# Sixteen transposes of a four-layer graph kernel: from TensorE to DMAs on ScalarE's queue

## What is computed

```
x = layernorm(x + L0(x, adj))   # adj @ (x @ W) + b, 8 heads of 32
x = layernorm(x + L1(x, adj))   # attention, 4 heads of 256
x = layernorm(x + L2(x, adj))   # two graph convolutions with relu
x = layernorm(x + L3(x, adj))   # relu(normalised adj @ x @ W)
# L1: ht = h @ W, src = ht . a_src, dst = ht . a_dst (per head)
#     e = leaky_relu(src[:, None] + dst[None, :]) + adj ; softmax(e) @ ht, mean of heads
```

## Time and profile before

| | us |
|---|---|
| median of 3 runs (lowest to highest) | 707.61 (707.03 to 707.86) |
| the profiled execution, its own time | 708.24 |
| its span on the core | 706.3 |
| PE busy in the span | 686.9 (97%) |
| DVE busy | 529.2 (75%) |
| ACT busy | 393.7 (56%) |
| POOL busy | 147.0 (21%) |
| mean granted clock of TensorE over the span | 0.995 |

### The profile page before, as it was taken

The page is one execution under the profiler, slowest core; times in us unless marked ns, Lnnn a source line. Parts: engine busy times, 40 slices in busy tenths (PEclk is TensorE's granted clock), DMA queues, the critical chain, the costliest instruction groups (busy, mean ns, idle before and its releaser), DMA issues.

```text
span 706.3 us, 16657 instructions
## 1 busy us (share of the span) xinstructions
PE 686.9 (97%) x5962; PEld 567.2 (80%) x5962; DVE 529.2 (75%) x988; ACT 393.7 (56%) x525; POOL 147.0 (21%) x236
## 2 busy tenths in 40 slices
PE   5989999999999999999999999999999999999996
PEld 4878854588888888888888888875677778888885
DVE  5788646999898979989899898998432325874564
ACT  6545146887989889798898989642100020123000
POOL 4965422000100000000000000653021102442222
PEclk9999999999999999999999999999999999999999
DMA  9986001001303012030300303013121000310011
GB/s 329 411 316 251 0 3 59 1 1 31 62 31 60 0 45 45 30 59 3 86 0 30 59 0 60 1 23 75 25 46 27 11 1 16 39 30 1 32 48 43
DMA packets 33147, 42.17 MB, mean 60 GB/s; under 512 B 21776, under 2 KB 27856, under 8 KB 30928
## 3 DMA queue, kind: packets, MB, share of 16 engines
q1 hardware_dynamic: 30528, 33.73, 14.8%
q0 software_dynamic: 2016, 7.34, 5.5%
q10 hardware_dynamic: 560, 0.52, 0.2%
HBM read 27.13 MB, written 2.13 MB: 41 GB/s over the span
## 4 chain that ended last, share of the span: by engine, by line
PE 84%; DVE 8%; POOL 4%; issue 1%; DMA 1%; ACT 1%; SPq 0%; POOLq 0%; DVEq 0%; ACTq 0%
PE ps L543 14%; PE ps L544 14%; PE ps L685 14%; PE ps L687 14%; PE ps L686 14%; PE ps L534 7%; PE ps L635 5%; DVE ring_hl L980 2%; DVE ring_a L975 2%; POOL x L1090 2%; POOL ring_a L1099 1%; DMA x<-in_x 1%; PE ps L499 1%; DVE x L753 1%; POOL ring_a L1111 0%
## 5 line engine op out<-in xcount | busy, mean ns | idle before, releaser
L687 PE MATMUL ps<-arena,ring_hl 128*128 (+1 forms) x1024 | 279.6, 273 | 0.0
L685 PE MATMUL ps<-arena,ring_hl 128*128 (+1 forms) x1024 | 278.8, 272 | 0.4 <-DVE ring_hl L980 0.4
L686 PE MATMUL ps<-arena,ring_hl 128*128 (+1 forms) x1024 | 278.6, 272 | 0.0
L543 PE MATMUL ps<-arena,adj 128*128 128x256 f16 (+1 forms) x1024 | 231.9, 273 | 0.6 <-issue 0.5
L544 PE MATMUL ps<-arena,adj 128*128 128x256 f16 x1024 | 232.1, 274 | 0.0
L975 DVE SCALAR_TENSOR_TENSOR ring_a<-rho,gam,ring_a 128x1024 f32<-128x1024 f32 x128 | 163.9, 1281 | 18.0 <-ACT ring_a L430 18.0
L980 DVE TENSOR_TENSOR ring_hl<-ring_a,ring_hl 128x1024 f16<-128x1024 f32 x128 | 156.7, 1224 | 6.0 <-ACT ring_hl L444 5.9
L444 ACT ACTIVATE ring_hl<-ring_a 128x1024 f16<-128x1024 f32 x128 | 135.3, 1057 | 44.2 <-PE ps L687 30.9
L430 ACT ACTIVATE ring_a<-adj,shift 128x1024 f32<-128x1024 bf16 x128 | 145.7, 1139 | 0.0
L543 PEld LDWEIGHTS ps<-arena,adj 128*128 (+1 forms) x1024 | 100.2, 98 | 18.5 <-issue 0.7
L544 PEld LDWEIGHTS ps<-arena,adj 128*128 (+1 forms) x1024 | 99.8, 97 | 16.4
(11 more groups left out here) (91 smaller groups left out, 566.8 us busy)
## 6 DMA issues: line engine op xcount, KB each, us to landing
arena<-in_adj SPq DMA_DIRECT2D x16, 1024.0 KB, 8.5
x<-y POOLq DMA_DIRECT2D x14, 512.0 KB, 5.2
rho<-s_scratch SPq DMA_DIRECT2D x8, 512.0 KB, 3.7
out_x<-x SPq DMA_DIRECT2D x16, 128.0 KB, 1.7
x<-in_x SPq DMA_DIRECT2D x3, 512.0 KB, 7.0
arena<-in_L_gnn_W SPq DMA_DIRECT2D x1, 1024.0 KB, 16.8
arena<-in_L_gnn_a SPq DMA_DIRECT2D x1, 1024.0 KB, 19.0
rho<-in_L_gnn_W SPq DMA_DIRECT2D x2, 512.0 KB, 10.2
```

The costliest lines, as they stand in the source:

```text
L543: nc.tensor.matmul(ps[:, bank, 0:width], lhs, pp[:, j, 0, 0:width], start=(j == 0), stop=False)
L685: nc.tensor.matmul(acc, hi, v_hi, start=(jt == 0), stop=False)
L686: nc.tensor.matmul(ps[:, b, 0:D], hi, v_lo, start=False, stop=False)
L687: ins = nc.tensor.matmul(acc, lo, v_hi, start=False, stop=(jt == T - 1))
```

## The change

The sixteen tiles of the second layer are no longer transposed on TensorE. ScalarE issues one DMA transpose for each tile, in order, each behind the low half of that tile's split, with one semaphore for each slot of `xs`; ScalarE's copies of the transposes are gone, and its casts stand between the issues (cast 7 ahead of the first one). TensorE's projections move from tile t - 5 to tile t - 7 in the steps of tile t (TURN_LAG = R + 3 = 7), so the aggregates of tiles 7 to 15 carry the projections of tiles 0 to 8, and seven are left, which go among the first six halves of the values as 1, 2, 1, 1, and one after each of the last two. VectorE's takes move from round t + 4 to round t + 7; those of tiles 9 to 15 stand after tile 15's split. VectorE's split of a tile waits for the DMA of four tiles before it in place of TensorE's transpose.

```diff
--- before.py
+++ after.py
@@ -154,6 +154,7 @@
         s_t, s_xt = sem("s_t"), sem("s_xt")
         s_td = sem("s_td")
         s_tc = [sem(f"s_tc{i}") for i in range(2)]
+        s_tg = [sem(f"s_tg{i}") for i in range(R)]
         s_w, s_ph, s_c = sem("s_w"), sem("s_ph"), sem("s_c")
         s_acc, s_sum = sem("s_acc"), sem("s_sum")
         s_deg, s_degp, s_dis, s_disw = sem("s_deg"), sem("s_degp"), sem("s_dis"), sem("s_disw")
@@ -211,10 +212,15 @@
             return adj[:, (n % 2) * JH:(n % 2 + 1) * JH, (n // 2) * LW:(n // 2 + 1) * LW], src
 
         EARLY = T - R - 1
+        TURN_LAG = R + 3
 
         def by_pe(k, t):
 
-            return k * T + t if k < 2 else 2 * T + (k - 3) * (T - EARLY) + t - EARLY
+            return t if k == 0 else T + (k - 3) * (T - EARLY) + t - EARLY
+
+        def gat_turned(t, u):
+
+            return s_tg[u], (t - u) * 4 + 16
 
         def conv_turned(t):
 
@@ -356,13 +362,12 @@
                     if t - AHEAD in between:
                         between[t - AHEAD]()
 
-            def lagged(k, first=0):
+            def lagged(k):
 
                 def one(t, u):
                     take_t(k, t, u)
-                    if k != 1:
-                        take_p(k, t, u)
-                tiles(act, first, T, one)
+                    take_p(k, t, u)
+                tiles(act, EARLY, T, one)
 
 
             def w1_hi(kk):
@@ -390,12 +395,14 @@
             nc.scalar.activation(w3[:, 0, :, :], w3f, ACT.Copy, scale=WS).then_inc(s_wh, 1)
             act.wait_ge(s_wa, 4 * K2)
             nc.scalar.activation(was[:, 0], wa[:, :, :, :], ACT.Copy, scale=WS).then_inc(s_wah, 1)
-            casts_after = {0: 7, 1: 9, 2: 11, 4: 13, 5: 15}
-            for t in range(R + 2):
-                take_t(1, t, t % R)
+            cast_n(7)
+            casts_after = {0: 9, 2: 11, 4: 13, 5: 15}
+            for t in range(T):
+                act.wait_ge(s_lo, T + t + 1)
+                act.dma_start_transpose(xt[:, t, :].rearrange("p (c i) -> p c i", c=2 * K2),
+                                        xs[:, t % R, :, :].rearrange("p q f -> p (q f)")).then_inc(s_tg[t % R], 16)
                 if t in casts_after:
                     cast_n(casts_after[t])
-            lagged(1, R + 2)
             act.wait_ge(s_turn, 1)
             act.wait_ge(s_wl, 3)
             nc.scalar.activation(srow, ps[0:SROWS, 7, 0:P], ACT.Copy).then_inc(s_sr, 1)
@@ -486,7 +493,7 @@
                 tiles(act, 0, EARLY - EARLY % R, lambda t, u: take_p(k, t, u))
                 for t in range(EARLY - EARLY % R, EARLY):
                     take_p(k, t, t % R)
-                lagged(k, EARLY)
+                lagged(k)
 
 
         @block.tensor
@@ -505,7 +512,9 @@
             def project(k, t, u):
                 if k == 0 and isinstance(t, int) and t == 0:
                     pe.wait_ge(s_wl, 1)
-                if k == 2:
+                if k == 1:
+                    pe.wait_ge(*gat_turned(t, u))
+                elif k == 2:
                     pe.wait_ge(*conv_turned(t))
                 elif k > 2 and not (isinstance(t, int) and t >= EARLY):
                     pe.wait_ge(s_td, by_dma(k, t))
@@ -579,17 +588,16 @@
             def rest(a, knext, ready):
 
                 k = (0, 2, 3, 4)[a]
+                back = TURN_LAG if knext == 1 else R + 1
 
                 def one(t, u):
                     pe.wait_ge(s_sum, t + (a * T - R + 1))
-                    prep = knext is not None and not (isinstance(t, int) and t == R)
+                    prep = knext is not None and not (isinstance(t, int) and t < back)
                     for j in range(T):
                         if j % JH == 0:
                             ready(t, u, j // JH)
-                        if j == T // 4 and prep and knext < 3:
-                            transpose(knext, t - R - 1, (u - 1) % R)
                         if j == (T - 2 if knext in (3, 4) else T // 2 + 2) and prep:
-                            project(knext, t - R - 1, (u - 1) % R)
+                            project(knext, t - back, (u - back) % R)
                         agg_step(a, k, t, u, j, j == T - 1)
                 one(R, 0)
                 tiles(pe, R + 1, T, one)
@@ -642,18 +650,16 @@
                     values_half(t, u, half)
 
             pe.wait_ge(s_wl, 5)
-            transpose(1, T - R - 1, R - 1)
-            transpose(1, T - R, 0)
-            for n in range(R):
+            left = list(range(T - TURN_LAG, T))
+            for n, count in enumerate((1, 2, 1, 1)):
                 pe.wait_ge(s_sum, T - R + n + 1)
                 values_half(n // 2, n // 2, n % 2)
-                project(1, T - R - 1 + n, (n - 1) % R)
-                if n < R - 1:
-                    transpose(1, T - R + n + 1, n + 1)
-            pe.wait_ge(s_xt, 2 * T - 1)
-            values_half(2, 2, 0)
-            project(1, T - 1, R - 1)
-            values_half(2, 2, 1)
+                for _ in range(count):
+                    tt = left.pop(0)
+                    project(1, tt, tt % R)
+            for n in range(2):
+                values_half(2, 2, n)
+                project(1, left[n], left[n] % R)
             pe.wait_ge(s_c, 2 * T)
             pe.wait_ge(s_idf, 1)
             nc.tensor.matmul(ps[0:SROWS, 7, 0:P], sd[:, 0, :, :].rearrange("p h t -> p (h t)"), ident_f[:, :],
@@ -808,8 +814,10 @@
 
                 def split():
 
-                    if k < 3:
-                        dve.wait_ge(s_t, t + (k * T - R + 1))
+                    if k == 1 and isinstance(t, int) and t < R:
+                        dve.wait_ge(s_t, T - R + t + 1)
+                    elif k == 1:
+                        dve.wait_ge(*gat_turned(t - R, u))
                     elif k == 3 and isinstance(t, int) and t < R:
                         dve.wait_ge(*conv_turned(t + T - R))
                     elif isinstance(t, int) and (t < R or t >= EARLY + R):
@@ -853,13 +861,14 @@
                     early, late_ = stages(a, k, t, u)[0], stages(a, k, t - 1, (u - 1) % R)[1]
                     if isinstance(t, int) and t == R:
                         late_ = []
-                    if k is not None and not (isinstance(t, int) and t == R and a > 0):
-                        late_.append(lambda: take(k, t - R, u))
+                    if k is not None and not (isinstance(t, int) and (t < behind or t == R)):
+                        late_.append(lambda: take(k, t - behind, (u - behind) % R))
                     if isinstance(t, int) and t in fill:
                         late_.append(fill[t])
                     for n in range(max(len(early), len(late_))):
                         for st in early[n:n + 1] + late_[n:n + 1]:
                             st()
+                behind = TURN_LAG if k == 1 else R
                 peeled = max(len(fill), 1)
                 for t in range(R, R + peeled):
                     one(t, t % R)
@@ -867,7 +876,7 @@
                 for st in stages(a, k, T - 1, R - 1)[1]:
                     st()
                 if k is not None:
-                    for t in range(T - R, T):
+                    for t in range(T - behind, T):
                         take(k, t, t % R)
 
             def sum_products(n):
```

## The result

| | before | after |
|---|---|---|
| median of 4 (lowest to highest), us | 707.74 (707.03 to 712.05) | 715.24 (712.08 to 717.31) |
| ratio to before, 95% interval | | 1.0094 [1.0075, 1.0113] |
| the profiled execution, its span | 708.24, 706.3 | 712.08, 710.1 |
| PE busy | 686.9 | 684.3 |
| mean granted clock | 0.995 | 0.992 |

Slower, as forecast, by more than forecast: the forecast was 712.0 in 709.3 to 714.2. The profiled execution is the fastest of the four. Thirteen executions of the changed kernel over several comparisons lie between 711.2 and 718.1, median 713.8; 69 of the kernel before lie between 706.9 and 712.1, median 708.4 (707.7 to 708.6 in the single comparisons). So two things ask for a reason: the step of 5.4 us between the medians, and a spread of 7 us.

A forecast was written before the change was run, and what follows sets the result against it. TensorE was taken to bound the kernel (84% of the chain), with VectorE's takes holding it after the change. Aggregates +0.7, tail +2.0 and clock +1.7 made 4.4 us: 712.6 profiled, 712.0 against the median, range 709.3 to 714.2.

The forecast's parts named there:

- The aggregates: Second layer's aggregates: projection 2 in tile 9 waits 6.2 us for VectorE's take 0; they end at 91.5, +0.7 us.
- No wait at 44: Sign in TensorE's timeline: the hole from about 44.2 to 46.5 us, before tile 0's transpose, goes, worth 2.3 us.
- The takes' order in the tail: Tail: projection 11 waits 1.5 us for take 9 behind tile 15's split; projection 15 starts 10.2 after the aggregates, +2.0 us.
- a fixed chain over VectorE, GpSimd and again VectorE: Tail, from projection 15 on: this chain frees the banks, and the values go on 5.2 us later.
- The clock: Behind the 6.2 us stand in tile 9 the clock falls: +1.7 us, bounds 0 and 2.6.
- the 475 to 480 row: Profile row of a stand of about 2.3 us that left the clock at 1.00, cited against a loss of clock.
- the clock falls twice: Rival: a second clock fall in the tail, behind stands of 1.5 and about 1.6 us; 1.7 more, 713.7; chance 0.13.
- The DMA lands late: Rival: tile 15's landing in the tail takes over 5.0 us instead of 2.4; 713.0 at 6 us; counted within the range.
- The high price: DMA landing beside adjacency loads: 12 us, from 4 x (1.19 + 1.9), against a low price of 2.4; hidden for tiles 0 to 8.

The follow-up runs named there:

- the lag alone: Kernel before, transposes still on TensorE, with projections and takes moved as in the changed kernel: 714.46 us, ratio 1.0084.
- takes a round sooner: Changed kernel with VectorE's takes one round earlier (t + 6, not t + 7), projections unmoved: 708.9 us, ratio 1.0005.
- the filler: Changed kernel with 52 matmuls into an unused PSUM bank ahead of projection 2 in tile 9: 711.38 us, ratio 1.0043.
- four banks: Changed kernel with second-layer projections in four PSUM banks in turn instead of two: 709.45 us, ratio 1.0034.
- the DMAs alone: Changed kernel with projections at t - 5 and takes in round t + 4, as in the kernel before: 712.92 us, ratio 1.0078.
- three banks: Changed kernel with tiles 0 to 7 transposed on TensorE, takes one round earlier, projections in three PSUM banks: 708.58 us, ratio 1.0004.
- the low half on VectorE: Tile 15's low half moved from GpSimd to VectorE: on the early-TensorE-tiles, three-PSUM-bank version 705.41 us (0.9952); on the kernel before 706.4 us (0.9976).

## Why the prediction was right and wrong

*The aggregates: right.* The sum came out as forecast and for the reason forecast. No wait at 44, a stand of 6.24 us (6.2 forecast) ending at 67.29 (67.4), put down to the take that stood at 67.00; TensorE arrived at 61.0 (61.2). With the clock the end of the aggregates was forecast 2.4 us later; it is 2.6 later, counted from the first sum. The kernel with the lag alone and the one with the takes a round sooner show that this is the cause.

*The takes' order in the tail: right in place, wrong in price.* This is one of the steps that failed. Projection 11 waits 1.54 us (1.5) and the last projection starts 103.26 - 92.90 = 10.4 us after the last aggregate (10.2). But I priced that at +2.0 because "a fixed chain over VectorE, GpSimd and again VectorE" was to follow projection 15 in 5.2 us. It is not fixed. In the kernel before 1.7 us of the 5.2 was GpSimd's all-reduce, which started 1.8 us after its data (99.85 to 101.68) and 5.62 us after GpSimd's low half; its row says "issue", not VectorE. After, the data come last (104.02, and the start is 104.15), 3.5 us lie between projection 15 and the ninth half, and TensorE does not stand at all. So the term is +0.4. The row of before was to be had; I read the chain's two ends and not the row between.

*The clock: the step that failed, together with the DMAs.* The sum had one loss of 1.7 us, in tile 9, which is near what the profiled execution has (2.71 us at work at 0.50 and 4 us at 0.88: 1.8). Against the filler it measured 1.7 to 3.0, and the bound was 2.6. The second loss, behind 480, stood in the sum at nothing, because the 475 to 480 row had shown the clock kept behind a stand of 2.3 us. That row does not hold for every execution: of 20 profiled executions, all with that same stand of 2.28 or 2.29 us, 9 fell to the low clock behind it and lost 1.7 us, and 11 kept it. One trace had shown one side. Of the five traces of the changed kernel four have this fall; of the two with the order of before neither has. Whether the change makes it more frequent, or whether this is chance, is open. The clock as a whole is lower after: the mean granted clock is 0.986 to 0.993 in the 13 executions of the changed kernel, and 0.995 or more in each of the 65 of the kernel before that have one on record. The rival "the clock falls twice", 713.7, is the pooled median (713.8) by luck: it put the second fall in the tail, where no trace of the changed kernel has one; I gave it 0.13.

*The DMA lands late: priced at nothing, on a bound that was wrong.* The high price for a landing beside the loads was 12 us, "hidden for tiles 0 to 8". The 1.9 us in it that stands for a load is the length of ScalarE's cast; the loads of the adjacency themselves took 4.7 to 14.8 us to land in the trace of before, 8.5 at the median. One DMA transpose landed after 20.2. What was not counted at all is that the load beside it comes late too and holds VectorE, whose takes are already what TensorE waits for, and that VectorE's split waits for a DMA transpose as well. If the counts are read right, this makes the executions above 715, two of the four that gave the median of 715.24.

*What the wrong terms did to the sum.* 0.7 + 1.7 in the aggregates (measured 2.6) and 2.0 in the tail (0.4) make 3.0 in place of 4.4. On the profiled 708.24 that is 711.2, which is the execution of 711.24, the one with no low clock at 480. The second low clock makes it about 713, a longer one in tile 9 714; the one traced late landing gave 718. The error of 1.6 us in the tail hid as much of this. The range was narrower above than its text says, too: its upper end, 714.2, is 0.5 us above the rival at 713.7 and not one. With one whole us it would have been 714.7, still below the 715.24.

*Open.* The first sum of the layer stands between 38.6 and 41.5 us in these traces, 39.1 in the one of before. That is 1 or 2 us of every single time, and I did not find what sets it. That a late landing makes all of the long executions is inferred from their counts and one trace, and what makes the long ones with the filler is not known.

## What to carry to other kernels

When work moves later on one engine, move the release of its buffer by less, or give it another buffer: here the projections went back two tiles and the takes three, and with two banks that one round cost 3.6 us of stand, and 4.9 us between the medians. Before an edit at the end of a stage is priced, read every row of the chain that follows, and what ended each wait: a span that looks fixed may be one engine's readiness, which hides a delay or gives a gain back. And one profile shows one side of a clock that may or may not fall: price such a stand on both sides.

## What the runs showed of the hardware

- GpSimd's all-reduce never started less than 5.5 us after GpSimd's last instruction ended: 5.62 before, 5.55 and 5.75 with four banks, 5.54 with the DMAs alone, 5.60 with takes a round sooner, 5.68 with three banks, each put down to issue, with the data there 1.1 to 2.5 us earlier. Where its data were later it started 0.13 us behind them (6.05 after). With the low half on VectorE (5.84 and 5.67) both limits are close, and the rows do not part them. Moving the instruction ahead of it gave 0.24% [0.10, 0.38] for itself, and a kernel at 0.9952 together with the earlier aggregates.
- DMA transposes beside loads that keep the DMA engines busy landed in 2.5 to 2.9 us at the median, but in 6.2 to 6.7 at worst in most traces and 20.2 in one, where a load beside them came late too (11.68 us of ScalarE's time). With only tiles 8 to 15 by DMA, behind most loads, the worst was 2.9 and 4.6.
- Behind the stand of 2.3 us near 480 the clock fell in 9 of 20 executions. Behind the stand of 2.26 or 2.27 us at 44 to 48 it fell in one trace (before) and not in two (the lag alone; before with the low half on VectorE). Behind stands of 2.6, 4.2, 6.0, 6.2 and 7.2 us it fell in all; behind 0.75 us, with the filler, in none of five, and behind 1.5 us in the tail in none of ten. Its stay at 1.2 GHz was not the same each time: 1.8 us lost in one execution, 3.0 in another with the same stand of 6.25.
